# Where TensorE loads the words of a round that begins behind a loop's jump

## The reference

```python
h = (x @ W).reshape(n, H, C)
a_src, a_dst = (h * att_src).sum(-1), (h * att_dst).sum(-1)
alpha = leaky_relu(a_src[src] + a_dst[dst])
m = segment_max(alpha, dst)                 # over the edges of one destination
e = exp(alpha - m[dst])
w = e / segment_sum(e, dst)[dst]
out = segment_sum(w[:, :, None] * h[src], dst)
```

## Time and profile before

| what | value |
|---|---|
| median of three runs | 6530.64 us |
| the profiled execution's own time | 6552.36 us |
| its span, first to last instruction | 6550.3 us |
| TensorE matmul busy | 4781.3 us (73%) |
| VectorE busy | 4564.3 us (70%) |
| GpSimd busy | 4532.0 us (69%) |
| ScalarE busy | 2734.9 us (42%) |
| mean granted clock of TensorE | 0.838 of full speed |

### The profile page before, as it was taken

How to read it: one execution, slowest core, us unless ns; L and a number is a source line. 1 busy time by engine, 2 the same in 40 slices (tenths; PEclk the granted TensorE clock), 3 DMA queues, 4 the chain that set the end, 5 groups by cost and what they waited for, 6 DMA issues and landing times. The chain is left out here.

```text
span 6550.3 us, 105533 instructions
## 1 busy us (share of the span) xinstructions
PE 4781.3 (73%) x21848; PEld 3433.9 (52%) x21849; DVE 4564.3 (70%) x13234; ACT 2734.9 (42%) x4932; POOL 4532.0 (69%) x4736
## 2 busy tenths in 40 slices
PE   6777777777777577777777777765776777677776
PEld 5555555555555455555555555544555555555555
DVE  6666666666666667777777777766766776677676
ACT  3343444344344334444444444433444444444443
POOL 2777777777777477767777777737777777777774
PEclk8788888888878778878887888877998999989898
DMA  8555555555555355555555555535555555555553
GB/s 271 146 149 150 148 152 147 149 149 149 148 148 150 99 150 163 162 155 159 160 159 158 162 159 159 162 105 150 158 156 152 153 156 156 149 156 154 153 154 97
DMA packets 477595, 1000.76 MB, mean 153 GB/s; under 512 B 143755, under 2 KB 284975, under 8 KB 476654
## 3 DMA queue, kind: packets, MB, share of 16 engines
q0 software_dynamic: 226208, 633.50, 36.6%
q1 hardware_dynamic: 250574, 356.73, 17.1%
HBM read 918.52 MB, written 71.30 MB: 151 GB/s over the span
## 5 line engine op out<-in xcount | busy, mean ns | idle before, releaser
L867 POOL DMA_INDIRECT e_rows<-table,loaded x4689 | 4513.6, 963 | 1883.7 <-issue 1670.9
L1160 PE MATMUL e_p_mm<-e_rows,e_onehot 128*128 128x264 f32 x9378 | 2762.9, 445 | 139.3 <-DVE e_rows L1354 109.2
L1160 PEld LDWEIGHTS e_p_mm<-e_rows,e_onehot 128*128 128x128 f32 x9378 | 1973.5, 219 | 555.4 <-issue 203.7
L1354 DVE TENSOR_TENSOR e_rows<-e_rows,e_p_pair 128x1024 f32<-128x1024 f32 x1173 | 1413.6, 1205 | 0.0
L1622 DVE TENSOR_TENSOR_SCAN e_fwd<-e_mask,e_p_one 64x128 f32<-64x128 bf16 (+1 forms) x294 | 121.9, 415 | 1294.4 <-PE e_p_one L1250 1294.4
L1346 DVE TENSOR_TENSOR e_onehot<-e_col,e_p_pair 128x512 f32<-128x512 f32 (+1 forms) x1176 | 903.1, 768 | 79.3 <-issue 76.1
L1250 PE MATMUL e_p_one<-ident,e_srcc 128*64 128x128 f32 (+1 forms) x294 | 91.2, 310 | 1006.9 <-issue 644.4
L997 ACT ACTIVATE e_onehotT<-e_onehotT,minus_pidx 128x2432 bf16<-128x2432 bf16 x294 | 680.8, 2316 | 21.2 <-DMA e_pass<-pass_rows 21.2
L1000 ACT ACTIVATE e_onehotT<-e_onehotT,one_col 128x2432 bf16<-128x2432 bf16 x294 | 682.6, 2322 | 9.6
L1250 PEld LDWEIGHTS e_p_one<-ident,e_srcc 128*64 128x64 f32 (+1 forms) x294 | 36.8, 125 | 1120.1 <-issue 1120.1
L1152 PE MATMUL e_p_mm<-e_rows,e_onehot 128*128 x1764 | 469.5, 402 | 208.9 <-DVE e_rows L1354 207.7
(11 more groups left out here) (323 smaller groups left out, 5384.7 us busy)
## 6 DMA issues: line engine op xcount, KB each, us to landing
e_onehotT<-rel_rows SPq DMA_DIRECT2D x294, 608.0 KB
e_rows<-table,loaded POOLq DMA_INDIRECT x4689
e_own_row<-table SPq DMA_DIRECT2D x196, 128.0 KB, 3.2
table<-e_rows_out SPq DMA_DIRECT2D x98, 132.0 KB, 2.7
table<-n_rows_out SPq DMA_DIRECT2D x14, 910.0 KB, 13.8
table<-e_rows_out SPq DMA_DIRECT2D x98, 130.0 KB, 3.0
n_inputs<-in_x_turned SPq DMA_DIRECT2D x14, 896.0 KB, 10.7
e_mask<-mask_rows SPq DMA_DIRECT2D x196, 64.0 KB
```

The lines of the kernel that those rows point to most:

```text
L867: pool.indirect_dma_start(rows[k][:, g, 0:TW], None, table[L], bass.IndirectOffsetOnAxis(ap=idx[k][:, g:g + 1], axis=0)).then_inc(s_gat[k] ...
L1160: ins = nc.tensor.matmul(p_mm[:, bass.ds(region, MW)], onehot[:, g, :], rows[k][:, g, :], start=False, stop=True, skip_group_check=True)
L1354: return nc.vector.tensor_tensor(feats, feats, p_e[:, gs, :].unsqueeze(3).to_broadcast([P, n, H, C]), ALU.mult)
```

## The change

In rounds of the loop with u = 0, and only there, TensorE's loads of the four groups of words come behind the turn of the scores and behind the carried block's product or the last sums. All other rounds are as they were, those that are written out too.

```diff
-                    if not first:
-                        regions = words(pe, REGION_ROW, (w - 1) * G, G, (REGIONS - 1) * BANK)
-                    offs = words(pe, AD_ROW, w * G, G, (PLACES - 1) * ADS_W)
-                    flag, *extra_ad = words(pe, WINDOW_ROW, w * WIN + W_FLAG, 1 + EXTRAS, (PLACES - 1) * ADS_W)
-                    slots = words(pe, WINDOW_ROW, w * WIN + W_TILE, EXTRAS, G - 1)
+                    def round_words():
+
+                        regions = None if first else words(pe, REGION_ROW, (w - 1) * G, G, (REGIONS - 1) * BANK)
+                        offs = words(pe, AD_ROW, w * G, G, (PLACES - 1) * ADS_W)
+                        flag, *extra_ad = words(pe, WINDOW_ROW, w * WIN + W_FLAG, 1 + EXTRAS, (PLACES - 1) * ADS_W)
+                        slots = words(pe, WINDOW_ROW, w * WIN + W_TILE, EXTRAS, G - 1)
+                        return regions, offs, flag, extra_ad, slots
+
+                    behind_jump = u == 0 and not isinstance(w, int)
+                    if not behind_jump:
+                        regions, offs, flag, extra_ad, slots = round_words()
                     def products(q):
 ...
                         last_sums(w, u, i)
                     if CARRY and finished(w, 7):
                         multiply(w, u)
+                    if behind_jump:
+                        regions, offs, flag, extra_ad, slots = round_words()
                     wait_apart(pe, st["scan"], now)
```

## The result

The change made the kernel slower. Over five runs of each on one chip the changed kernel takes 6560.97 us (median, 6559.66 to 6565.01), the kernel before 6527.23 (6525.75 to 6537.1): ratio 1.005, 95% interval 1.0035 to 1.0064, or 34 us more. 6517 was predicted, with a range of 6486 to 6556. The profiled execution took 6562.96, its span 6560.7. One execution of the version with a loop that begins at round 18 took 12,202 us at a granted clock of 0.316 and is left out; all ratios are of the others.

The account below looks back on a forecast made before the run. It took TensorE's issue time before the turn behind loop jumps, which holds up GpSimd's gathers, as the bound. Gains of 31 us, less 8 for first rounds and 9 for clock, gave 14: 6530.6 to 6517, range 6486 to 6556.

Parts of the forecast that it names:

- turn earlier: Behind a jump, the scores' turn starts earlier by means of 3.4, 4.2, 4.0 us in layers 0, 1, 2, capped by the loads' time.
- turn to row sums: From turn to line 1259: 0.6 us of issue (0.9 in layer 2), 4.0 of loads, 0.15 for two waits.
- row sums to products(0): Line 1259 to products(0): 3.04 us, 16 lookups being issue-bound again, with the branch and three lookups following.
- products(0) to extra products: Stretch behind products(0): the clock was to cost 1.4 us in half of layer 2's rounds, nothing in layers 0 and 1.
- first rounds, all three: Each layer's loop round entered without a jump gains nothing at the front and loses 3.2, 2.1, 3.0 us: 8 together.
- W = 4.0: Time TensorE's sequencer takes to load the 39 words, in us; by likelihood 3.5 to 4.9.
- The stretch of 5.8: From the start of the extra products to the next turn, in us: upper end for the loads, including issue of seven products.
- "3.2" behind the words: Time in us from the end of the word loads to products(0): 0.15 for two waits plus 3.04.
- The clock ... I count half of the 13 rounds: Layer 2's products(0) run cold, 3.88 instead of 2.50 us, in half of 13 rounds: 9 us lost.
- C: Rival: slower, lookups come too late behind the words; 6549 us, deciding from a load time of 4.6; chance 0.25.
- B: Rival: the loads go quite out of the way, covered by the cold product; 94 us gained, 6437; chance 0.05.
- D: Rival: no change, 6530 us; the gathers' 20.0 set the loop's period, or gain and first rounds' loss cancel; chance 0.28.

Follow-up runs that it names:

- second profile of before: The kernel before, unedited, run and profiled once more: 6528.23 us, ratio 1.0002, its profiled execution 6525.9.
- 16-word version: Against the kernel before, behind a jump only the 16 region words are loaded behind the product, the other 23 ahead of the turn: 6505.41 us, ratio 0.9968.
- most words a round early: The 16 region words behind the product behind a jump; without a jump, the 23 other words a round early: 6473.04 us, 0.9923 to the kernel before.

## Why the prediction was wrong

Its steps, beside what the traces of the changed kernel and of the second profile of before hold (us a round; gains are positive):

| step | predicted | measured |
|---|---|---|
| turn earlier | 3.35, 3.95, 3.85 | 3.16, 3.96, 3.82 |
| turn to row sums | 4.75, 4.75, 5.05 | 5.25, 5.26, 5.38 |
| row sums to products(0) | 3.04 | 3.30, 3.25, 3.22 |
| turn to products(0), now | 4.72, 4.78, 5.45 | 4.75, 4.79, 5.29 |
| gain at products(0) | 0.25, 0.9, 1.2 | -0.64, 0.24, 0.51 |
| products(0) to extra products | 0, 0, -0.7 | -0.50, -0.04, -1.41 |
| a layer's 13 rounds | 3, 12, 7 | -14.8, 2.6, -11.7 |
| first rounds, all three | -8 | -9.1 |
| sum | 14 | -33 |

The measured sum agrees with the 34 us between the medians, in part by luck: with the first profile of before as its base the same sum gives -22. It was made as the forecast was, from distances alone, and the layers changed one by one bear it out (18, -3 and 13 us slower by the ratios, 18, 0 and 15 by the distances), so the mechanism was right: what is taken at the front against what comes back behind it, one for one. Three of its terms were mis-sized, and each gain was a small difference of such terms.

**"W = 4.0."** It is 4.45, inside the 3.5 to 4.9 that were given. "No row shows them" was wrong: loads of registers have no rows in the timeline, but the view of a source line lists them. Line 136 of the kernel before holds the four loads between the products and the turn of the earlier trace rows; line 824 holds the loops' jumps (ns: min/median/max; then first and last start):

```profile
L136 PEldq TENSOR_LOAD <-off_row x4: 512/1032/1364, 1563.4 to 1567.1; - x4
L824 PEldq COMPARE_BRANCH  x42: 76/4180/5094, 521.7 to 6458.6; - x42
```

From the first load to the end of the last are 4.5 us there and 4.2 behind a jump, with the arithmetic on addresses ahead of them and between them 4.4 to 4.6. The stretch of 5.8 had room for this: the sequencer's work for seven products takes 0.9, from 1562.4 to 1563.3, 0.12 each and not the 0.2 that the sum took. And the 3.7 us by which the idle time behind a jump is longer is the jump itself, 4.2 us in the median, which no order of the loads changes. By the 200 ns per register of the Trainium skill, Runtime: NRT & Kernel Launch, section Instruction fetch mechanics, 39 words would be 7.8. The measured 4.45 / 39 is 0.11 a word, and the trace doesn't agree; the Trainium skill gives its figure there for the register loads that the runtime puts in, and these are the kernel's own.

**"3.2" behind the words.** Two waits and 3.04 were taken from an ordinary round, where the sequencer had been waiting for the scans and had some lead on the array. Behind 39 words it has none: from row sums to products(0) are 3.2 to 3.3. With W, this is 0.75, 0.71 and 0.50 a round, 13 x 1.96 = 25.5 us, of which about 17 are W's and 8 those of the lookups' stretch. That the missing lead makes this last difference of 0.2 is argued; the 16-word version shows only that a lead is worth 0.74 to 0.81 in layers 0 and 1, where the row sums stayed and products(0) came later.

**"The clock ... I count half of the 13 rounds", and 0 in layer 0.** Granted clock, third column from the end, of the changed kernel: products(0) of round 30 of layer 2, then products(1) behind two jumps of layer 0 (rounds 24 and 54):

```profile
5087.43:5090.80 3.37, 3.37 (x9) 2.41 (x9) 0.82 (x3) 0.83 (x2) 2.65 (x3) 0.58 0.61 231
...
664.64:667.57 2.93, 2.93 (x10) 2.11 (x8) 2.59 (x6) 0.00 (x0) 2.32 (x3) 0.67 0.59 148
...
1304.89:1306.87 1.98, 1.98 (x10) 1.44 (x8) 1.87 (x5) 0.00 (x0) 1.68 (x2) 1.00 0.61 190
```

The same product of layer 2 in the first profile of before:

```profile
5081.34:5083.84 2.50, 2.50 (x9) 1.86 (x10) 2.46 (x6) 2.47 (x2) 1.89 (x3) 0.81 0.79 187
```

In this round products(0) of layer 2 run at 0.58 instead of 0.81, 1.2 GHz for most of their time. Over the 13 rounds the mean is 0.52, where the second profile of before has 0.98, and none of them runs above 0.6: from their start to that of line 1281 are 3.75 on average, where they were 2.01. The size was right (1.4 a round predicted, 1.41 measured at the extra products), the number of rounds was not: 13 x 0.71 = 9.2 us more. In layer 0 the cold stretch now reaches into products(1) in every other of these rounds (2.8 to 3.0 us instead of 2.05), 0.5 on average, 6.5 us. Those are also the rounds in which GpSimd waits 4.5 to 4.7 behind the extra products; in the others it is 2.3 to 2.8.

Together 25.5 + 9.2 + 6.5 = 41.2. The rest of the 47 is in small terms: 2.5 from the front of layer 0 (3.16 and not 3.35), 2.1 from products(0) of layer 2 in the kernel before (5.29, not 5.45; the first profile has 5.39), 1.1 from the first rounds, 0.5 from layer 1's last stretch, so 47.4. Taking the terms from an execution 25 us above the median added a part of these last ones, and no more.

**The rivals.** C is what happened: words too late, products(0) of layer 2 cold in every round. It was put at 6549 and said to decide from W = 4.6; it decided at 4.45, because the 0.2 behind the row sums and the clock of layer 0's products(1) were missing from it too. B fell: 3.5 of the 4.45 lie bare in a warm round. D's mechanism, that the gathers set the period whatever TensorE does, isn't seen in the rounds behind a jump, where each layer paid its own distances; in the ordinary rounds of layer 0, which won 0.4 us each with most words a round early and got no shorter, it stays open.

## What to carry to other kernels

Loads moved off a front come back in full where the next user of the words stands, and once more as the lead which the sequencer had there: move only those whose user is far (the 16 region words, 0.32% faster), or load a round ahead (0.8% together with those 16), and not those that the very next burst needs. A load that is put behind one burst still holds whatever the sequencer issues behind it, as layer 2 shows. When a gain is 0.2 to 1.2 us between terms of 3 to 8, a term's error of 10% decides its sign; read the term first where the trace has it, here in the view of the source line that makes the loads, or measure it with a version that has only the term in it.

## What the runs showed of the hardware

One batch ran on a chip on which the kernel before takes 10,048 us (33 runs, 10,039 to 10,063) instead of 6527, with the same packets and bytes moved. Waits of the kernel with only layer 2 changed, on that chip:

```profile
DVE e_adst L1670 <- remote: 3536.2, 283, 32.0
POOL e_rows L867 <- PE e_p_mm L1152: 3251.8, 241, 32.8
```

VectorE waits 12.5 us a round behind the lookups for something that the profile can only call remote, and GpSimd's wait for line 1152 is 20 times what it was. The cause stays open. Ratios of that batch don't carry over, distances on one engine's sequencer do: with only layer 0 changed its row sums come 5.18 and products(0) 8.49 behind the turn there, 5.25 and 8.55 at 6541 us.

Two profiled executions of one kernel, 6552.4 and 6525.9, differ by 0.4%, where the whole effect in question is 0.5%.

Behind a jump a load of 16 words into TensorE's registers takes 1.1 to 1.3 us, one of four words 0.51 and one of three 0.78; a jump of the loop takes 4.0 to 4.2 us in the median, 0.08 where the loop ends and it isn't taken.
